# Last chunk of a local attention stage: key projections in other PSUM banks, a second buffer for the key parts, and new order tables for all engines

## The reference, cut to what matters

```python
x = x + _L0_attn_a_ref(_layernorm(x), w_qkv, w_out, pos_bias, scale_embed, if_gain)  # 44 fixed offsets back in time
x = x + _L0_ffn_ref(_layernorm(x), W1, b1, W2, b2)                                   # 8 groups of 512 tokens, linear
x = x + _L0_attn_b_ref(_layernorm(x), Wqkv, Wo)                                      # full softmax attention with rotary
x = x + _L0_ffn_ref(_layernorm(x), W1, b1, W2, b2)
# attention b: q = q * cos + rotate_half(q) * sin, the same for k; softmax(q k / 4) v; 16 heads of 16
```

## Time and profile before

| | |
|---|---|
| median of three runs | 2423.65 us |
| the profiled execution | 2422.75 us |
| its span (first to last instruction) | 2421.1 us |
| TensorE / DVE / ACT / POOL busy, share of the span | 94% / 80% / 65% / 32% |
| mean granted TensorE clock, share of full speed | 0.977 |
| `local_stage` in the trace | 0 to about 861 us |
| `full_attention` | about 861 to 2320 us |

### The profile page before, as it was taken

The page is one execution under the profiler, slowest core; times in us unless marked ns, Lnnn a source line. Parts: engine busy times, 40 slices in busy tenths (PEclk is TensorE's granted clock), DMA queues, the critical chain, the costliest instruction groups (busy, mean ns, idle before and its releaser), DMA issues. The chain is left out here.

```text
span 2421.1 us, 48160 instructions
## 1 busy us (share of the span) xinstructions
PE 2281.9 (94%) x14400; PEld 865.8 (36%) x14400; DVE 1938.0 (80%) x2283; ACT 1567.5 (65%) x3608; POOL 780.7 (32%) x1019
## 2 busy tenths in 40 slices
PE   7899999999967689999999999999999999999988
PEld 5444555455533232333323332333333333333233
DVE  4777999999958568888888888888888888888545
ACT  0346666666643167777777777777777777777841
POOL 2789999999951034020020020020000000041100
PEclk9999999999988799999999999999999999999999
DMA  8355767675685079050050050050000000031221
GB/s 287 107 120 110 157 151 155 143 167 129 150 154 113 22 124 104 10 72 5 3 72 5 3 72 4 3 72 3 4 20 3 5 20 3 5 98 35 68 99 52
DMA packets 235188, 177.17 MB, mean 73 GB/s; under 512 B 153287, under 2 KB 204823, under 8 KB 235079
## 3 DMA queue, kind: packets, MB, share of 16 engines
q1 hardware_dynamic: 199132, 113.20, 20.1%
q0 software_dynamic: 16480, 43.52, 11.5%
q10 hardware_dynamic: 19472, 19.12, 2.7%
HBM read 110.29 MB, written 48.31 MB: 66 GB/s over the span
## 5 line engine op out<-in xcount | busy, mean ns | idle before, releaser
L1344 ACT ACTIVATE pr<-ps_s 128x512 f32<-128x512 f32 x2048 | 1114.6, 598 | 332.7 <-PE ps_s L1271 308.7
L1358 DVE TENSOR_REDUCE mx<-ps_m 128x1 f32<-128x1024 f32 x980 | 1154.1, 1219 | 218.1 <-PE ps_m L1242 211.8
L1271 PE MATMUL ps_s<-qs,ks 99*128 (+1 forms) x2048 | 701.9, 382 | 15.5 <-SPq L1143 6.5
L1242 PE MATMUL ps_m<-ks,qs 96*128 (+1 forms) x1960 | 586.0, 380 | 0.2 <-issue 0.2
L1280 PE MATMUL ps_o<-pr,vg 128*32 128x512 f32 x4096 | 545.5, 605 | 0.2
L551 POOL TENSOR_TENSOR qs<-ks 128x512 f32<-128x512 f32 x336 | 425.3, 1298 | 74.5 <-ACT ks L795 51.5
L1271 PEld LDWEIGHTS ps_s<-qs,ks 99*128 (+1 forms) x2048 | 195.5, 96 | 648.4 <-issue 425.2
L1185 POOL DMA_DIRECT2D vg<-vb_d x24 | 19.6, 817 | 1166.3 <-PE ps_o L1280 1076.1
L1242 PEld LDWEIGHTS ps_m<-ks,qs 96*128 (+1 forms) x1960 | 189.8, 98 | 173.8 <-issue 10.2
L870 DVE TENSOR_TENSOR ks<-PSa,ks 128x512 f32<-128x512 f32 x368 | 231.9, 678 | 10.6 <-PE PSa L636 7.9
L636 PE MATMUL PSa<-ks,sj 128*32 128x512 f32 x736 | 194.3, 603 | 3.0 <-DVE ks L870 1.9
(11 more groups left out here) (186 smaller groups left out, 2039.6 us busy)
## 6 DMA issues: line engine op xcount, KB each, us to landing
qs<-skew SPq DMA_DIRECT2D x128, 208.0 KB, 4.0
ks<-k_d POOLq DMA_DIRECT2D x48, 256.0 KB, 9.3
qs<-q_d POOLq DMA_DIRECT2D x180, 64.0 KB, 9.3
skew<-attn SPq DMA_DIRECT2D x64, 164.0 KB, 4.6
tail_room<-in_W SPq DMA_DIRECT2D x32, 256.0 KB, 3.4
tail_room<-in_W2T SPq DMA_DIRECT2D x32, 256.0 KB, 4.0
vb_d<-vb SPq DMA_DIRECT2D x8, 1024.0 KB, 6.9
qs<-ks SPq DMA_DIRECT2D x26, 256.0 KB, 4.7
```

Source lines behind the costliest of these rows:

```text
L1242: mm = pe.matmul(ps_m[:, u % 2, kc * CH:(kc + 1) * CH], qs[0:KROWS, bass.ds(nq, 1), j, qt * P:(qt + 1) * P].rearrange("p a t -> p (a t)"), ...
L1271: pe.matmul(ps_s[:, op % SB, :], ks[0:KROWS + PARTS, bass.ds(slot, 1), j, kt * P:(kt + 1) * P].rearrange("p a t -> p (a t)"), qs[0:KROWS + ...
L1344: act.activation(pr[:, kt % 4, j, :], ps_s[:, op % SB, :], ACT.Exp, scale=HD ** -0.5).then_inc(p_ready, 1)
L1358: dve.tensor_reduce(mx[:, j * TILES + qt, half:half + 1], ps_m[:, u % 2, :], AX_X, ALU.max).then_inc(m_read, 1)
```

## The change

It makes four edits in `local_stage`:

1. In chunk 7 the key projections (`qk` 1) and their rotations use banks 4 and 5 in place of 6 and 7. `qk` 1 then waits for nothing, and `values` waits for the two query rotations only.
2. In chunk 7 the three parts of the key go to a second buffer, `qparts_last`, in room that held the scores. Their first write no longer waits for the query's stores; it waits until DVE has made the query's last part (`qparts_ready`), since that frees the fp32 copy.
3. The 12 query loads of the first group are a step of their own, `ahead_q` 0 to 5; `ahead_load` keeps the six key loads. Each kind waits for less than both did: the query loads no longer wait for the products.
4. All ten order tables are new.

```diff
+        qparts_last = q_room[:, 10240:11776].bitcast(BF16).rearrange("p (a s n) -> p a s n", a=2, s=PARTS)
...
+        def parts(j, i):
+            return (qparts_last if j == NG - 1 and i >= 2 else qparts)[:, i % 2]
+
+        def qk_banks(j, i):
+            return TURN_BANK if j == NG - 1 and i else TAIL_BANK
...
             def ahead_load(n):
                 if n == 0:
+                    pool.wait_ge(prod_d_used, NG * N_DVE)
+                    pool.wait_ge(prod_p_ready, NG * N_POOL)
+                rows = slice(HD * n, HD * (n + 1))
+                pool.dma_start(ks[rows, 0, :, :], D["k_d"][K_STACK[n], :, 0:GRP, CH:CH + T]).then_inc(ahead_ld, 16)
+
+            def ahead_q(n):
+                if n == 0:
                     for s in range(2):
                         pool.wait_ge(qparts_stored[s], 32 * NCH)
-                    pool.wait_ge(prod_d_used, NG * N_DVE)
-                    pool.wait_ge(prod_p_ready, NG * N_POOL)
                     pool.wait_ge(fold_stored, 32 * NG)
...
-                    else:
+                    elif j < NG - 1:
                         pe.wait_ge(qkb_read, 4 * j + 2)
...
-                        mm = project(PS[:, TAIL_BANK[half], :], wqkv_b[:, :, u * P:(u + 1) * P], tn.xm)
+                        mm = project(PS[:, qk_banks(j, i)[half], :], wqkv_b[:, :, u * P:(u + 1) * P], tn.xm)
...
-                    pe.wait_ge(qkb_read, 4 * j + 4)
+                    pe.wait_ge(qkb_read, 4 * j + (4 if j < NG - 1 else 2))
...
-                    act.copy(qparts[:, i % 2, 0, :], rope_q[:, i % 2, :]).then_inc(rope_high, 1)
+                    act.copy(parts(j, i)[:, 0, :], rope_q[:, i % 2, :]).then_inc(rope_high, 1)
...
-                    need(dve, qparts_stored[i % 2], j * 32 + 16 * (i // 2))
+                    if j == NG - 1 and i >= 2:
+                        dve.wait_ge(qparts_ready, j * 4 + i - 1)
+                    else:
+                        need(dve, qparts_stored[i % 2], j * 32 + 16 * (i // 2))
```

More of the change, by code:

```diff
@@ L104 @@
+    (34.906, "far", 6), (40.512, "far", 7)]
 PE_STEPS = [
[L105 to L108 removed]
@@ L221 @@
-ONCE = {"fold_load": 0, "fold": 0, "fold_out": 0, "gain": 0, "ahead_load": NG - 1, "ahead": NG - 1, "ahead_rows": NG - 1}
+    (-189.084, "fold", 0), (-176.937, "fold", 1), (-160.247, "fold", 2), (-139.999, "fold", 3), (-139.164, "fold_out", 0),
+    (-137.421, "fold", 4), (-132.878, "fold", 5), (-121.503, "fold", 6), (-116.028, "fold", 7), (-116.027, "fold_out", 1),
+    (-113.748, "fold", 8), (-89.292, "fold", 9), (-89.103, "fold", 10), (-86.161, "fold", 11), (-85.776, "fold_out", 2),
+    (-80.008, "fold", 12), (-78.82, "fold", 13), (-68.926, "fold", 14), (-63.556, "fold", 15), (-63.226, "fold_out", 3),
@@ new lines @@
+    (-63.225, "fold", 16), (-59.563, "fold", 17), (-54.422, "fold", 18), (-31.441, "fold", 19), (-30.679, "fold_out", 4),
+    (-11.251, "h_mean", 0), (-10.687, "fold", 20), (-8.198, "h_var", 0), (-7.634, "fold", 21), (-6.81, "h_back", 0),
+    (-5.755, "k", 0), (-4.802, "q", 0), (-4.487, "fold", 22), (-4.108, "fold", 23), (-1.094, "v", 0), (-0.608, "fold_out", 5),
+    (3.322, "v", 1), (4.203, "k", 1), (7.829, "q", 1), (8.578, "fold", 24), (9.049, "fold", 25), (12.199, "logits", 0),
+    (15.334, "logits", 1), (15.899, "fold", 26), (18.294, "logits", 2), (18.605, "fold", 27), (18.911, "fold_out", 6),
@@ new lines @@
+DVE_STEPS = [
+    (-272.989, "fold", 0), (-137.751, "fold", 1), (-49.228, "fold", 2), (-29.11, "fold", 3), (-29.109, "fold_out", 0),
+    (-27.116, "fold", 4), (-24.078, "fold", 5), (-10.56, "h_add", 0), (-10.507, "fold", 6), (-9.553, "fold", 7),
+    (-9.552, "fold_out", 1), (-9.459, "fold", 8), (-9.277, "fold", 9), (-9.15, "fold", 10), (-8.999, "fold", 11),
+    (-8.998, "fold_out", 2), (-8.994, "fold", 12), (-8.93, "fold", 13), (-8.799, "fold", 14), (-8.705, "fold", 15),
+    (-8.704, "fold_out", 3), (-8.698, "fold", 16), (-8.583, "fold", 17), (-8.538, "fold", 18), (-8.516, "fold", 19),
+    (-8.515, "fold_out", 4), (-8.514, "h_center", 0), (-7.35, "h_inverse", 0), (-5.908, "h_normalise", 0),
+    (-4.289, "fold", 20), (-2.98, "fold", 21), (-2.744, "fold", 22), (-0.808, "fold", 23), (1.515, "fold", 24),
+    (1.559, "fold_out", 5), (5.558, "fold", 25), (12.017, "fold", 26), (12.873, "fold", 27), (14.151, "soft", 0),
+    (16.404, "weights", 0), (17.1, "soft", 1), (20.002, "soft", 2), (20.301, "weights", 1), (21.777, "fold", 28),
+    (23.043, "soft", 3), (23.047, "weights", 2), (24.732, "weights", 3), (25.092, "fold_out", 6), (25.6, "fold", 29),
+    (25.642, "soft", 4), (26.377, "fold", 30), (26.536, "fold", 31), (28.072, "soft", 5), (28.385, "weights", 4),
+    (29.152, "gain", 0), (29.725, "soft", 6), (31.38, "weights", 5), (32.959, "weights", 6), (34.712, "soft", 7),
+    (36.117, "weights", 7), (40.429, "fold_out", 7), (45.962, "add", 0), (46.165, "t_add", 0), (46.846, "t_center", 0),
+    (49.232, "t_inverse", 0), (49.379, "t_normalise", 0), (50.82, "update", 0), (51.223, "t_add", 1), (51.973, "t_center", 1),
+    (53.915, "t_inverse", 1), (54.806, "t_normalise", 1), (58.261, "rotate", 0), (58.524, "rotate", 1), (59.293, "rest", 0),
+    (59.798, "rest", 1), (60.307, "last", 0), (61.323, "last", 1), (63.491, "rotate", 2), (64.094, "rotate", 3),
+    (66.977, "rest", 2), (71.781, "rest", 3), (73.34, "last", 2), (74.425, "last", 3)]
@@ L222 @@
+ONCE = {"fold_load": 0, "fold": 0, "fold_out": 0, "gain": 0, "ahead_load": NG - 1, "ahead_q": NG - 1, "ahead": NG - 1, "ahead_rows": NG - 1}
 PIECES = 4
@@ L586, in _ @@
                     ahead_load(i)
+                elif what == "ahead_q":
+                    ahead_q(i)
                 else:
@@ L843, in step @@
                     dst = QKD[i // 2][:, (i % 2) * (HD // 2):(i % 2 + 1) * (HD // 2), :, (j + 1) * CH:(j + 2) * CH]
[L844 removed]
+                    act.dma_start(dst.rearrange("s d h t -> (d h) s t"), parts(j, i)).then_inc(qparts_stored[i % 2], 16)
                 elif what == "values":
@@ L969, in step @@
                 elif what == "rotate":
-                    low, high = (PS[:, TAIL_BANK[h], :] for h in ((1, 0) if i % 2 else (0, 1)))
+                    low, high = (PS[:, qk_banks(j, i // 2)[h], :] for h in ((1, 0) if i % 2 else (0, 1)))
                     dve.wait_ge(angle_ld, 32 * j + 32)
```

228 lines of the change are left out of this document (99 added, 129 removed).

## The result

| | before | after |
|---|---|---|
| median, four runs each | 2424.47 us | 2386.32 us |
| range | 2419.4 to 2431.79 | 2383.45 to 2387.81 |
| ratio, 95% interval | | 0.9829, 0.981 to 0.9849 |
| profiled execution: span | 2421.1 us | 2386.1 us |
| mean granted TensorE clock | 0.977 | 0.981 |

The account below looks back on a forecast made before the run. TensorE's own pace bounds chunks 1 to 7; after chunk 7's last product DMA, DVE's maxima, then a chain of single steps. Terms -9.5 - 9.6 + 3 + 0 - 5 + 3 = -18.1 us give 2404.7 us, range 2390 to 2427.

Parts of the forecast that it names:

- End of the stage: Chunk 7's end: key projections follow at once, last key store lands at 851.1 against 860.6; -9.5 us.
- Maxima ahead of `add`: Chunk 7 on DVE: 68 in place of 84 maxima stand ahead of `add`; -9.6 us.
- waited for no DMA: Chunk 7's last `turn`, 61 us after the skew-load stretch, waited for no DMA; argument against the skew rival.
- Inside the norm: Chunk 7's first norm: eight maxima ahead of `t_inverse` and four ahead of `t_normalise` lengthen it; +3 us.
- the pair ahead of `update` is free: Chunk 7's first norm: the pair of maxima ahead of `update` lies in a 5.00 us gap and costs nothing.
- Query loads as a step: Chunk 7's loads: same transfers and bytes, delays covered by other work; 0 us, bounds -3 and +5.
- skews gate the last chunk: Rival, chunk 7: later skew loads delay the last `turn`, so the moved maxima win nothing; -8.5 us, 2414 us; 15%.
- `fold_out` 7: TensorE's idle stretch from 160 to 200 us: DVE's step moved behind TensorE's part removes its wait; -5 us.
- Chunk 0: First chunk: put at nothing, 0 us, though its order tables are new.
- The steady chunks: Six chunks: only P16, P17 between `h_var` and `h_back` cost half a microsecond each; +3 us.
- third rival: DVE becomes the bound in every chunk through closer norm steps; +41 in place of +3, 2443 us; 13%.
- fixed mark at 718: Chunk 7 after its last product: the DMA stretch holds the second tile to 718 us anyway.

Follow-up runs that it names:

- e9: Changed kernel with the values' store split in two halves, issued earlier, and the row of ones loaded earlier; ratio 0.9811 to the kernel before.
- e5: Kernel before with only TensorE's and DVE's changed order from chunk 7's last turn to the second norm (fewer maxima ahead of `add`); ratio 0.9948.
- e6: Changed kernel with the old order from the last tile's turn to the second norm, 84 of 88 maxima ahead of `add`; ratio 0.9858 to the kernel before.
- e10: Changed kernel with six of the twelve maxima inside chunk 7's first norm moved on, six now ahead of `update`; ratio 0.9825 to the kernel before.
- e8: Changed kernel with the query loads merged back into the six load steps; ratio 0.9828 to the kernel before.
- e3: Kernel before with only the query loads split off and POOL's new order in chunk 7; ratio 0.9975.
- e13: Kernel before with only DVE's part of `fold_out` 7 moved three slots back; ratio 0.9998.
- e14: Kernel before with the norm steps at every chunk's head as late as in the changed tables, two slots apart; ratio 1.0174.

## Why the prediction was wrong in size

**End of the stage, -9.5: mis-sized, -6.** The mechanism held step by step: projections at once, passes at 0.43 us from 805 us on, a key store last. The step that failed is "Its store is issued at 848.3 and lands at 851.1". The issue came 19.4 us behind the start of the projections (I had 19.1), and the values' store 4.1 us ahead of it, also as worked out. But that store takes 5.9 us, the two overlap, and for the key store I took a landing measured without it. In e9, with the values' stores out of the way, the last key store lands in 2.9 us.
The Trainium skill ("TensorE: Matmul & The Clock Gate", What's actually happening) has the clock slow by default and released by activity; the trace agrees, 0.86 us a pass for the first 4.4 us of the block and 0.43 behind it.

**Maxima ahead of `add`, -9.6: -11 to -14** (e5, e6), right as a mechanism and somewhat short. The whole stretch gave -15.5; the rest came with other steps, perhaps the shorter skew wait of the `turn` at 755.54 us. My "waited for no DMA" was true of the last `turn` and not of that one. **Inside the norm, +3: +3.0 to +3.8**, right. That the pair ahead of `update` is free was right for one and wrong for three (e10).

**Query loads as a step, 0: right for edit 3 by itself in the changed kernel (0 to 3 us, e8), wrong on the kernel before (-5 to -7, e3) and for the stretch, -9.** The step that failed is "under the DMA stretch that holds its tile to 718 anyway". I took a queueing delay as a fixed mark, although its sign stood in my rows: a load of 208 KB that took up to 28.1 us, issued in the middle of 2.3 MB. The trace of before had the order of the issues, and the diff had what the new tables did to `weights` 1 and to the fifth and sixth load. My rival "skews gate the last chunk" had the sign the wrong way round: what it feared for tiles 2 to 5 happened to tile 1, as a gain.

**`fold_out` 7, -5: the size of chunk 1's gain is about right by luck, the reason wrong.** The wait of 10.7 us was the longest of DVE, and removing it is worth nothing (e13). What wins in chunk 1 is open. **Chunk 0, 0:** some -4.6 in the mean of the profiles, a term that I put at nothing without a reason.

**The steady chunks, +3: -2 to -5.** The step that failed is "`h_var` and `h_back` now have only P16, P17 between them". There is also `values`, 3.7 us, which stands there in both kernels. Moved alone, the steps cost what my third rival says: I had +41, measured is +42 (e14). That the two numbers agree so well is partly luck: at `h_inverse` and `h_normalise` DVE waits 19.0 us in five chunks of e14, 3.8 a chunk, where the rival has 6.9. I gave it 13% and did not look at what else stood between the two steps. Why the changed kernel does not pay is open between `values` and the places of `logits` 2 and `soft` 2. (The rival's "from 5 us a chunk on" is too high as well: the other terms give -21.1, so the sign turns at 3.5.)

The spans differ by 35.0 us, 16.9 more than forecast: 9.1 for the stretch of the loads, 5.9 for the maxima, 6.7 for the steady chunks with chunk 7's products and 0.3 for the rest of the kernel, less 1.2 for chunk 1, 0.8 for the norm and 3.2 for the end. So the largest failed step is the fixed mark at 718.

## What to carry to other kernels

A long wait for a DMA is not a fixed date: find out what else was issued around the transfer, because one step moved ahead in DVE's queue took it from 28 to 7.5 us. Price an order by what stands between two dependent steps in time, with every other step counted, not in slots; the same distance of two slots went with a loss of 42 us in one kernel and with none in another. And a wait that is the longest of its engine may be worth nothing: take it away alone before it gets a price. A stretch that one profile shows unchanged may still have changed: compare several.
